# Feature-value products directly ahead of the next key features, and another order and bank plan of the FFN part

## The reference

```python
x1 = x + xattn(layernorm(x), ctx_2048)          # 16 heads of 32, 64 features
    q, k, v = LN(x) @ Wq.T + bq, ctx @ Wk.T + bk, ctx @ Wv.T + bv
    q' = relu(q @ Wqf.T);  k' = relu(k @ Wkf.T) * mask
    kv = einsum('bhnf,bhne->bhfe', k', v);  k_sum = k'.sum(n)
    out = (q' @ kv) / (q' @ k_sum + 1e-8);  return out @ Wo.T + bo
y = x1 + ffn(layernorm(x1))
    gate, up = bit_linear(x, w_gate), bit_linear(x, w_up)      # activations to 8 bits, weights to -1, 0, 1
    a = subln(up * relu(gate)**2, subln_weight);  return bit_linear(a, w_down)
```

## Time and profile before

| | us |
|---|---|
| median of 3 runs | 430.47 (430.22 to 432.01) |
| the profiled execution, whole | 431.65 |
| its span, first to last instruction | 429.6 |
| TensorE (PE) busy | 411.4 (96%) |
| VectorE (DVE) busy | 342.3 (80%) |
| ScalarE (ACT) busy | 286.5 (67%) |
| GpSimd (POOL) busy | 145.8 (34%) |

### The profile page before, as it was taken

One profiled execution on the slowest core, in us unless ns is written; L12 is line 12 of the kernel. 1 busy time (PEld: TensorE's weight loads), 2 busy tenths in 40 slices (PEclk: granted clock), 3 DMA queues, 4 the chain that ended last, 5 costly groups with the idle time before them and its releaser, 6 DMA issues.

```text
span 429.6 us, 11266 instructions
## 1 busy us (share of the span) xinstructions
PE 411.4 (96%) x4804; PEld 284.4 (66%) x4835; DVE 342.3 (80%) x505; ACT 286.5 (67%) x406; POOL 145.8 (34%) x290
## 2 busy tenths in 40 slices
PE   8989999999999999999989999999999999999995
PEld 4879899988878945844754575575567566464443
DVE  4644659658679959899986897999998798998982
ACT  5655989892155287778449747765873878939960
POOL 0000000003054722483371545547325523344660
PEclk9989999999999999999999999999999999999999
DMA  7992474632050300113323033031213021413065
GB/s 235 418 403 74 169 278 159 287 120 82 24 198 5 108 19 2 32 31 87 73 38 63 0 88 76 11 75 50 51 41 70 14 50 27 84 62 75 1 146 124
DMA packets 51170, 42.42 MB, mean 99 GB/s; under 512 B 43056, under 2 KB 44080, under 8 KB 49200
## 3 DMA queue, kind: packets, MB, share of 16 engines
q1 hardware_dynamic: 51120, 41.70, 32.9%
HBM read 27.01 MB, written 4.19 MB: 73 GB/s over the span
## 4 chain that ended last, share of the span: by engine, by line
PE 52%; DVE 21%; issue 7%; ACT 7%; POOL 6%; DMA 6%; SPq 0%; DVEq 0%; ACTq 0%
PE ps L538 11%; PE ps L407 11%; PE ps L358 6%; PE ps L360 5%; PE ps L359 5%; PE ps L555 4%; DVE zb L974 3%; PE ps L429 2%; PE ps L514 2%; DMA xqT<-xqb 2%; PE ps L448 2%; DVE rows_of L922 2%; DVE tk L985 2%; DVE qol L933 1%; DVE rows_of L917 1%
## 5 line engine op out<-in xcount | busy, mean ns | idle before, releaser
L538 PE MATMUL ps<-tg,xqT 128*128 128x512 bf16 x243 | 58.1, 380 | 4.6 <-DMA xqT<-xqb 2.9
L538 PE MATMUL ps<-tu,xqT 128*128 128x512 bf16 x245 | 59.1, 379 | 1.3 <-issue 0.6
L555 PE MATMUL ps<-td,yqT 128*128 128x512 bf16 x202 | 45.9, 379 | 1.1 <-DMA yqT<-yqb 0.7
L538 PEld LDWEIGHTS ps<-tg,xqT 128*128 128x128 bf16 x256 | 23.5, 98 | 33.1 <-DMA xqT<-xqb 4.0
L538 PEld LDWEIGHTS ps<-tu,xqT 128*128 128x128 bf16 x256 | 24.2, 98 | 31.2 <-issue 3.0
L721 ACT ACTIVATE rb<-zb 128x1024 f32<-128x1024 f32 x29 | 30.6, 1055 | 20.7 <-DVE zb L974 20.5
L974 DVE TENSOR_TENSOR zb<-ps,rb 128x1024 f32<-128x1024 f32 x29 | 35.3, 1218 | 8.2 <-ACT rb L717 8.0
L358 PE MATMUL ps<-aph,wqh 128*128 128x256 f32 x128 | 37.2, 290 | 0.0
L360 PE MATMUL ps<-aph,wkl 128*128 128x256 f32 x124 | 35.4, 286 | 1.8 <-issue 1.8
L985 DVE TENSOR_REDUCE tk<-zb 128x1 f32<-128x1024 f32 x30 | 36.2, 1207 | 1.0 <-POOL zb L1189 0.7
L358 PE MATMUL ps<-aph,wkh 128*128 128x256 f32 x124 | 36.2, 292 | 0.6 <-issue 0.6
(11 more groups left out here) (153 smaller groups left out, 1037.1 us busy)
## 6 DMA issues: line engine op xcount, KB each, us to landing
xs<-in_wg_dram SPq DMA_DIRECT2D x4, 1024.0 KB, 13.9
xs<-in_wu_dram SPq DMA_DIRECT2D x4, 1024.0 KB, 6.6
xs<-in_wd_dram SPq DMA_DIRECT2D x4, 1024.0 KB, 7.9
xs<-in_x_dram SPq DMA_DIRECT2D x8, 512.0 KB, 4.9
out_dram<-xs SPq DMA_DIRECT2D x15, 256.0 KB, 2.0
craw<-in_ctx_dram SPq DMA_DIRECT2D x7, 512.0 KB, 5.8
xs<-in_wk_dram SPq DMA_DIRECT2D x4, 256.0 KB, 5.0
xs<-in_wv_dram SPq DMA_DIRECT2D x4, 256.0 KB, 6.6
```

Source lines behind the costliest of these rows:

```text
L538: k = pe.matmul(ps[:, b0 + n, :], xqT[:, i % 3, kc, :], tern[w][:, o:o + 512], start=kc == 0, stop=kc == KC - 1)
L555: k = pe.matmul(ps[:, D_BANK[i], :], yqT(i)[:, j, :], tern[2][:, 512 * j:512 * j + 512], start=j == 0, stop=j == 15)
```

## The change

TensorE runs the same 190 stages in another order. `key_values(b)` now stands directly in front of `key_features(b+1)` for b = 0 to 5, behind both halves of `values(b+1)`, and writes banks 6 and 7 (which `keys(b+1)` used); `keys(b+2)` waits for its two copies. `key_values(6)` stands in front of `query_features(0)`. `total(0)` is followed by `values(2, 0)`, and `total(1)` by `key_values(2)`, each with a wait for its mean. In the FFN part `up` has a bank table of its own (`U_BANK`), gates, ups, downs, projections and the feature stages use all eight banks, and several stages change places by one or two. The lists of ScalarE, VectorE and GpSimd are ordered anew; VectorE gives `weighted(26)` to GpSimd and `scaled_y` 4, 6, 28 and `rounded_y` 4, 10, 12, 31 to ScalarE, and takes `weighted` 5, 14, 20 and `rounded_y` 3, 13, 17, 22. GpSimd has `x_bias(4)` and `(5)` behind `x1_step(0)`. SyncE has `load_small` ahead of `load_context(1, 0)`, and a few stores and turns change places by one.

The core of the diff:

```diff
-KV_BANK = (0, 0, 0, 0, 0, 0, 0, 6)
+KV_BANK = (6, 6, 6, 6, 6, 6, 6, 6)
...
-G_BANK = (0, 0, 0, 0, 0, 0, 0, 0, 0, 0, 0, 0, 0, 0, 0, 0, 0, 0, 0, 0, 0, 0, 0, 0, 0, 0, 0, 4, 0, 4, 0, 4)
...
+G_BANK = (6, 4, 4, 0, 0, 0, 0, 4, 6, 6, 6, 6, 0, 0, 0, 4, 4, 0, 0, 4, 4, 4, 4, 4, 4, 6, 4, 6, 0, 6, 0, 4)
+U_BANK = (0, 0, 2, 2, 4, 4, 4, 0, 0, 2, 2, 2, 6, 6, 2, 6, 2, 2, 2, 2, 6, 6, 6, 6, 2, 4, 0, 4, 2, 4, 2, 6)
...
-            keys(1); values(1, 0, range(12), v_rows.at(0, 0)); key_values(0); values(1, 1, range(12))
-            key_features(1, (0, kvc_rows.at(0, 0)), (1, kvc_rows.at(0, 1))); keys(2); total(0); key_values(1)
-            values(2, 0, range(12), w_mean.at(0)); values(2, 1, range(12))
-            key_features(2, (0, kvc_rows.at(1, 0)), (1, kvc_rows.at(1, 1))); keys(3); key_values(2); values(3, 0, range(12))
-            values(3, 1, range(12)); total(1); key_features(3); keys(4, w_mean.at(1)); key_values(3)
...
-            values(7, 0, range(4), v_rows.at(6, 0)); transpose(1); values(7, 0, range(4, 12)); key_values(6)
-            values(7, 1, range(6)); queries(0, 0); queries(0, 1); query_features(0); values(7, 1, range(6, 12))
...
+            keys(1); values(1, 0, range(12), v_rows.at(0, 0)); values(1, 1, range(12), v_rows.at(0, 1))
+            key_values(0, kT_rows.at(1, 1), kT_rows.at(1, 3)); key_features(1)
+            keys(2, kvc_rows.at(0, 0), kvc_rows.at(0, 1)); total(0); values(2, 0, range(12), w_mean.at(0))
+            values(2, 1, range(12)); key_values(1, kT_rows.at(2, 1), kT_rows.at(2, 3)); key_features(2)
+            keys(3, kvc_rows.at(1, 0), kvc_rows.at(1, 1)); values(3, 0, range(12), v_rows.at(2, 0))
+            values(3, 1, range(12), v_rows.at(2, 1)); total(1); key_values(2, w_mean.at(1)); key_features(3)
+            keys(4, kvc_rows.at(2, 0), kvc_rows.at(2, 1)); values(4, 0, range(12)); values(4, 1, range(12))
...
+            values(7, 0, range(4, 12)); queries(0, 0); queries(0, 1); values(7, 1, range(6), qT_rows.at(0, 1))
+            key_values(6, qT_rows.at(0, 3)); query_features(0); values(7, 1, range(6, 12)); attend(0, (0, qf_rows.at(0, 1)))
...
+            key_values_copy(1, 0); scaled_weights(0, 3); key_values_copy(1, 1); magnitudes(1, 0); context_hi(4, 0)
...
-            x1_var(0); x1_rstd(0); x_bias(4); x_bias(5); x1_step(0); step_cubed(0); x1_weight(0); x1_weight_squared(0)
...
+            x1_var(0); x1_rstd(0); x1_step(0); step_cubed(0); x_rstd(5); x1_weight(0); x1_weight_squared(0); x_bias(4)
```

More of the change, by code:

```diff
@@ new lines, in tensor @@
+            keys(5, kvc_rows.at(3, 0), kvc_rows.at(3, 1)); total(2); values(5, 0, range(12)); values(5, 1, range(12))
+            key_values(4, kT_rows.at(5, 1), kT_rows.at(5, 3)); key_features(5, (2, w_mean.at(2)))
+            keys(6, kvc_rows.at(4, 0), kvc_rows.at(4, 1)); values(6, 0, range(12), v_rows.at(5, 0))
+            values(6, 1, range(12), v_rows.at(5, 1)); key_values(5, kT_rows.at(6, 1), kT_rows.at(6, 3)); key_features(6)
+            values(7, 0, range(4), v_rows.at(6, 0)); transpose(0, kf_rows.at(6, 0)); transpose(1, kf_rows.at(6, 1))
@@ L623, in scalar @@
+            down_last()
         def scalar(act):
@@ L798, in scalar @@
+            relu(14); relu_squared(14); transposed_hi(10); sum_of_squares(14); relu(15); transposed_hi(11); scaled_y(13)
+            rounded_y(12); relu_squared(15); sum_of_squares(15); scaled_x(8)
+            for n in range(4):
+                query_rows(5, n)
             for n in range(4):
                 query_feature_rows(5, n)
-            relu_squared(16); inverse_root(5, 0); inverse_guess(5, 0); scaled_x(9); sum_of_squares(16); relu(17)
-            relu_squared(17); inverse_root(5, 1); inverse_guess(5, 1); attended_hi(5, 0); sum_of_squares(17)
@@ new lines, in scalar @@
+            sum_of_squares(22); scaled_x(12); relu(23); query_rows(7, 0); query_rows(7, 1); relu_squared(23); rounded_y(20)
+            scaled_y(21); query_rows(7, 2); query_rows(7, 3); sum_of_squares(23); relu(24); rounded_y(21); relu_squared(24)
+            for n in range(3):
+                query_feature_rows(7, n)
+            sum_of_squares(24); query_feature_rows(7, 3); scaled_x(13); inverse_root(7, 0); inverse_guess(7, 0)
+            inverse_root(7, 1); inverse_guess(7, 1); relu(25); relu_squared(25); attended_hi(7, 0); attended_hi(7, 1)
@@ L1191, in gpsimd @@
             set_ones(); set_constants(); weight_product()
-            for n in range(12):
+            for n in range(5):
                 x_rstd(n)
@@ L1199, in gpsimd @@
+            for n in range(6, 12):
                 x_rstd(n)
-            square_sum(0); variance(0); y_rstd(0); y_weight(0); x1_var(2); x1_rstd(2); x1_step(2); step_cubed(2)
-            x1_weight(2); x1_weight_squared(2); y_most(0); y_steps(0); out_scale(0); factor(0); x_bias(6); square_sum(1)
-            variance(1); y_rstd(1); y_weight(1); x_bias(7); x1_var(3); x1_rstd(3); y_most(1); y_steps(1); out_scale(1)
-            x1_step(3); factor(1); step_cubed(3); x1_weight(3); x1_weight_squared(3); weighted(5); square_sum(2)
@@ new lines, in gpsimd @@
+            y_most(2); y_steps(2); out_scale(2); factor(2); weighted(7); x1_var(4); x1_rstd(4); square_sum(3); variance(3)
+            y_rstd(3); x1_step(4); y_weight(3); step_cubed(4); x1_var(5); x1_rstd(5); y_most(3); y_steps(3); x1_weight(4)
+            factor(3); x1_step(5); x1_weight_squared(4); out_scale(3); step_cubed(5); x1_weight(5); x1_weight_squared(5)
+            x_bias(8); x_bias(9)
+            for n in range(12, 16):
+                x_rstd(n)
+            weighted(9); square_sum(4); variance(4); y_rstd(4); y_weight(4); y_most(4); y_steps(4); factor(4); out_scale(4)
```

426 lines of the change are left out of this document (213 added, 213 removed).

## The result

The changed kernel takes 456.08 us (median of four runs, 450.75 to 457.28) where the kernel before took 430.35 beside it: a ratio of 1.057, 95% interval 1.052 to 1.061. It is slower by 25.7 us. The ratios in this document leave out one execution of 1049.23 us among the twelve of the kernel with the order of before and the FFN part of after; it counts in that kernel's median of 428.34, and no trace shows why it was so long. The profiled execution has a span of 455.3 us, which is also 25.7 above the 429.6 of before, so the two traces can be set against each other stage by stage.

The account below looks back on a forecast made before the run. The prediction took TensorE's instruction supply, in blocks of 256, to bound the kernel's first third. Its terms summed to +17.05, which with the profiled 429.6 and 0.87 to the median gave 447.5 us, range 433 to 455 (0.79).

Parts of the forecast that it names:

- seven stops in the merged bursts: Merged key_values/key_features bursts: TensorE waits for instruction blocks, four of 2.0 and three of 3.3 us beside bulk loads, +17.9.
- stops elsewhere: The two late stops of the kernel before, 0.57 and 0.36 us, fall away: -0.9.
- the clock: Behind the seven stops: one in three brings a fall of the granted clock, 1.3 us each, +2.6; bounds 0 and +9.
- fewer bursts entered and left, first attention: TensorE: 37 burst islands in place of 43, -1.2; query_features(0) no longer waits for the query rows, -0.6.
- totals: Stages behind total(0) and total(1) wait for w_mean, 0.4 and 0.85 us: +1.25; bounds 0 and 2.
- first gate's wait: First gate: its 0.82 us wait for xqT goes as x_bias(4), (5) move behind x1_step(0): -1.0; bounds -1.0 and 0.
- FFN part to `down(11)`: FFN part: engine work shifts nearly evenly and some xqT waits change; taken as -1.0, bounds -3.5 and +3.
- tail behind `down(11)`, without the clock: Tail: keeps its chain from gate(15, 1) to down_last, so its 2.5 us of wait stay.
- more falls of the clock: Key stages behind stops: every stop of 2 us or more drags a slow one, up to +6.5, 454 us; no separate chance.
- No limit on the fetch: Merged bursts: blocks can be asked for earlier or two at once, nothing starves; 427.7 us, chance 0.12.
- Half of it: Merged bursts: only waits without bulk load, no clock fall, or some bursts better placed; 7 x 1.2, 435.4 us, chance 0.13.
- The balance of VectorE: FFN part: no starvation, but VectorE's new weighted makes three gates or ups 1.2 us late; +3.6, 432.3 us, chance 0.06.

Follow-up runs that it names:

- the pairs alone: Kernel before with only the six pairs key_values(b), key_features(b+1), their banks and the ScalarE order they need; FFN part as before: 449.50 us, ratio 1.044.
- the two load experiments: Changed kernel, loads of x(2) to x(5) behind query_features(0): 455.11 us, single run; same plus the old tail and up weights behind key_features(2): 452.13 us, ratio 1.049.
- the old tail: Changed kernel with scaled_y(28), rounded_y(31) back on VectorE, weighted(28) ahead of gated(30), first-half turn of y(14) ahead of a store: 453.56 us, ratio 1.050.

## Why the prediction was right

The prediction said slower by starvation, 447.5 us in a range of 433 to 455; it came out slower by starvation at 456.08, 1 us past the range's end. The mechanism was the right one; 8.6 us are missing from the sum, 5.5 of them in the term of the clock. Term by term, on the profiled executions:

| term | predicted | measured |
|---|---|---|
| seven stops in the merged bursts | +17.9 | +17.5 |
| stops elsewhere | -0.9 | -0.9, +1.2 (new, at 115.1), +0.2 (the first) |
| the clock | +2.6 | +7.2 ahead of the first gate, +0.9 in the tail |
| fewer bursts entered and left, first attention | -1.8 | -1.5, as the remainder |
| totals | +1.25 | +1.3 |
| first gate's wait | -1.0 | -0.8 |
| FFN part to `down(11)` | -1.0 | -2.7 |
| tail behind `down(11)`, without the clock | 0 | +3.3, of which the late turn is 1.9 |

*Stops.* The sum is right, and in part by luck, since the sizes are less so. The four pairs that were taken as free of bulk loads have 1.5 to 2.3 where 2.0 was said, but one of them, `key_values(3)` with `key_features(4)`, has the load of the down weights beside it: 2.31, and 4.39 with the pairs alone. Of the three with one, `key_values(1)` and `(6)` have 4.4 and 4.6 where 3.3 was said, but `(4)` has 1.1, with another 1.2 behind it. A load costs 2.2 to 2.6 us, as the two load experiments show (in one of them the stop of 4.58 vanished whole), not 1.3; the 1.3 was read from one block, with no larger case in the trace of before. The places were right: 126 instructions into `key_features(1)`, said 128; the seventh one instruction pair before `query_features(0)`.

*The clock* is the mis-sized term that counts most. "One in three of seven" was taken from three stops, of which one was followed by a fall. After, five of the new stops had one: the stages behind them are longer by 1.4, 1.6, 1.0, 1.0 and 2.2 us, 7.2 in all. A sixth fall, in the tail, cost some 0.9. This was the rival of more falls of the clock, of which 5.5 of its 6.5 us came, and it was given no chance of its own. It stays open what decides on a fall. The length of the stop doesn't: in the run without bulk loads beside the pairs, stops of 1.67, 1.73, 2.09 and 2.86 us have no fall behind them. The key stages there:

```profile
37.84:43.40 5.56, 5.56 (x55) 5.56 (x49) 2.55 (x5) 0.84 (x2) 0.00 (x0) 1.00 0.11 43
...
94.48:100.24 5.76, 5.76 (x59) 5.76 (x50) 2.55 (x5) 1.25 (x4) 0.00 (x0) 1.00 0.01 3
```

The first of these follows the stop of 1.67, where the changed kernel, after one of 1.70 at the same instruction, took 7.19. Falls that come in one execution and not in the next also fit the wide spread of the four runs, 450.75 to 457.28, where the granted clock goes from 0.981 to 0.963.

*The stop at 115.1* was missed, since only multiples of 256 in bursts were looked at. It is one block after the stop at 110.11, in `keys(6)`. Two things come together there. No packet in any run starts less than 3.2 us after the one before, so a late one delays the next. And between 110.11 and the start of this block's packet at 112.71 the DMA engines had a share of 0.83, beside the load of Wo; that is 2.6 us, where the next packet started 1.1 to 1.2 us behind the stops at 76.84, 94.06 and 128.21. No run took that load away, so their shares are not shown.

*Totals.* 0.82 for the wait of `key_values(2)` on `w_mean(1)`, said 0.85, and about 0.5 for the first, said 0.4.

*FFN part.* The gain was there and larger than said in these two traces (2.2 and 2.7), less in the one with the old tail (0.9). The tail was said to stay, because its chain of stages was the same. That step failed: the chain was the same, but not the engines and buffers beside it. The reassignment of `rounded_y(31)` to ScalarE stood in the diff, and the prediction counted its busy time only, not the buffer that it waits for. The wait for this buffer and the slower `weighted(28)` together cost 1.4 us in the two kernels with the changed tail and an early turn; the 1.9 of the late turn and the 0.9 of the clock came on top in this execution.

*The signs.* The stops came where they were said to, five of the six in `key_features` at 1.5 us or more. `keys(4)` starts 11.5 us later, not 8, the first gate 24.2 and not 17 to 18, and from there to the end it takes 1.5 us more and not 1 to 2 less; the clock and the larger stops are in the first two, the tail in the last.

*The rivals.* No limit on the fetch (427.7) is refuted by the stops. Half of it (435.4) too, since they came to 17.5 us where it had 8.4. The balance of VectorE was no bound in the body of the FFN part of the changed kernel; its costly place was the tail. (Two of the variants have a wait of 1.13 us for VectorE in an `attend`.)

## What to carry to other kernels

Read the waits that have no name: when TensorE stops with nothing to wait for, count its instructions from one stop to the next, and look for the packet of the instruction queue ahead of each. Where stages of very short matmuls issue hundreds of instructions in a few us, put long matmuls between them, and keep bulk loads from starting in the moment that the next block is asked for; 6 matmuls of 0.23 us took 1.5 to 2.5 us from four of five stops. When an order is undone to find its price, undo the lists of the other engines with it, and look at what a load moved out of the way makes late.

## What the runs showed of the hardware

Where TensorE stood waiting for it, a block of 256 instructions was usable 2.2 to 2.7 us after its packet had started, whatever the DMA engines carried meanwhile (shares of 0.00 to 0.99); the one exception is 3.5 us, at the stop of 1.28 in `key_features(5)` of the pairs alone. What varied was when the packet started, counted from the instruction 264 ahead of the stop: 0.5 to 2.2 us in the bursts where the DMA engines carried little in between (share of up to 0.2), 2.7 to 5.1 where a bulk load ran in the second pair or `key_values(6)`; in `key_features(5)`, beside the loads of x(0), x(1) and Wo, it ranges from 0.6 us ahead of that instruction to 4.0 behind it. No two packets of this queue started less than 3.2 us apart in any run, while 256 instructions of a burst last 1.3 to 1.5 us: a burst of 512 runs ahead of its supply even beside idle DMA engines.

The stop near 23 us, at the same instruction, lasted 0.8 to 2.3 us in kernels that are nearly alike up to there. That may be part of why runs of one kernel differ by 2 us and more; a profile of several runs of one kernel, which would show it, was not made.

VectorE's product zb by g_b of 128 x 1024 took 3.17 us beside the same kind of product on GpSimd, and 1.22 us with the old tail, where it ends as GpSimd's begins. In the first case GpSimd's had begun 0.28 us earlier and took its usual 2.36. At 402.4 in the same trace VectorE's began 0.47 us ahead of GpSimd's; there it took 1.22 and GpSimd's 3.01. So the one that began first took its usual time and the other waited. The product that follows in the old tail, with one operand in PSUM, lies beside GpSimd's (2.37 us) and still takes 1.22.
